# Products of two constants into an unread PSUM bank, in the table stages, the relational output and the attention outputs

## The chip, the cores and the metric

One NeuronCore of a Trainium2 chip runs the whole program. The metric is the device time of one execution in microseconds (us); lower is better.

## The reference

Four graph layers follow each other on 3125 nodes of width 32 and 100000 edges that are sorted by destination. Each layer is added to its input and layer-normalised:

```python
x = _layernorm(x + _L0_gnn_ref(x, Wq, Wk, Wv, Wo, edge_index))        # attention over edges, 4 heads
x = _layernorm(x + _L1_gnn_ref(x, weight, w_comp, self_loop_weight,
                               A1_w, A1_b, A2_w, A2_b, rel_emb, src, dst, edge_type))   # 86 relations, 16 bases
x = _layernorm(x + _L2_gnn_ref(x, edge_weight, src, dst, 3))          # three rounds of weighted sums
x = _layernorm(x + _L3_gnn_ref(x, edge_index, ..., Wl, bl, Wr, br, att, ...))   # 3 GATv2 layers, 8 heads of 32
```

In the layers that look at pairs of nodes, each node is first projected: `xl = x @ Wl + bl` for the source side and `xr = x @ Wr + br` for the destination side. For a GATv2 layer these are 8 x 32 = 256 columns each; the output of such a layer is the mean over heads of `sum(alpha * xl[src])`.

## The kernel before

The program is a sequence of stages. Each stage is a block in which every engine has its own list of instructions; engines wait for each other by semaphores, and the next stage begins when all engines have finished the block. The 3125 nodes lie as NB = 25 blocks of 128 nodes (the partitions). All orders below are written out by hand; there is no scheduler.

**Table stages** (`tables`, run five times: t, r, g0, g1, g2). TensorE (PE) transposes x four blocks at a time (`turn`, line L497, a product with the identity into `psT`), ScalarE (ACT) copies the result to `XT` (L514), and then for each block PE makes two f32 products of `XT` with the weights (L506): the source side into one half of `psA` and the destination side into the other, two blocks in turn. ACT copies the first half to `big` (L2005, L1461, L1992). The second half goes to `rows`, by VectorE (DVE) in stages t and r (L2006, L1459), by ACT in g0 to g2 (L1993). SyncE sends `big` to HBM in four parts (L545). In g0 to g2 DVE follows with `self_logits`: for every four blocks it adds the two sides (L1823), makes the leaky ReLU (L1809), multiplies by the attention vector (L1812) and reduces (L1815), and at the end it subtracts once for all blocks (L1829). The contraction of the products is 33 rows (32 features and a row of ones), 32 rows in stage t. Widths are 64 and 32 columns in t, 32 and 32 in r, 264 and 264 in g0 to g2. An f32 product is two instructions of PE in the trace.

**Relational output** (`relational_out`, once). For each block PE transposes four 128x128 parts of the sums and one of 32 columns into `psA` (L1422, L1424), one block ahead; ACT copies them to `work` (L1445, L1446); PE multiplies them with `w1b` and `w1s`, 32 columns wide, into `psC` (L1434, L1436); DVE takes the result (L1452).

**Attention output** (`attention_out`, once in each of g0 to g2). DVE computes the normalising factors (L1854 to L1866) and signals `shifted` after L1858. It then forms the normalised sums in four parts of 6, 6, 6 and 7 blocks (L1870, L1871, L1873), each part signalling `sums`. PE works on pairs of blocks: `turn` transposes the pair's four 128x128 parts into `psT` (L1904), ACT copies them to `work` (L1889), PE multiplies by `w3o`, 32 columns wide, into `psC` (L1916), ACT copies that out (L1880). `turn` runs one pair ahead.

Between the table stage and the output of each layer lie the edge stages (`logits`, softmax, weighted sums). They are not changed. The stage `dense_fill` of the third layer already issues, after each of its products (L1669), a 128x512 bf16 product of `ident_b` with `iota_b` into a bank that nobody reads (L1671).

Of the kernel before, what the change touches and what calls it, by code (L numbers as in the profile page):

```python
# [468 lines left out]

def tables(nc, m, name, sources, dests, tab, side, layer=None):

    gat = layer is not None
    w = m.table_d[name].shape[1]
    out = m.big[:, 0:NB * w].rearrange("p (b w) -> p b w", b=NB)
    rows = sources.shape[0]
    steps = [range(b, min(b + 4, NB)) for b in range(0, NB, 4)]  # L480
    parts = 4
    ends = [(n + 1) * NB // parts for n in range(parts)]

    def bank(b, n):
        return m.psA[:, b % 2, n * 512:n * 512 + (sources, dests)[n].shape[1]]

    with ExitStack() as ctx:
        s = Stage(nc, f"tab_{name}")
        block = ctx.enter_context(nc.Block())

        @block.tensor
        def _(pe):
            def turn(n):
                need(pe, s("copied"), n - 1)
                for b in steps[n]:
                    at = (b - steps[n][0]) * P
                    ins = nc.tensor.transpose(m.psT[0:D, n % 2, at:at + P], m.X[:, b, :], m.ident[:, :])  # L497
                ins.then_inc(s("turned"), 1)
            turn(0)
            for b in range(NB):  # L500
                if b % 4 == 0 and b // 4 + 1 < len(steps):
                    turn(b // 4 + 1)
                pe.wait_ge(s("copied"), b // 4 + 1)
                for n, (weights, read) in enumerate(((sources, "tab"), (dests, "side"))):
                    need(pe, s(read), b - 1)
                    nc.tensor.matmul(bank(b, n), m.XT[0:rows, b * P:(b + 1) * P], weights, start=True,  # L506
                                     stop=True).then_inc(s(f"made_{read}"), 1)

        @block.scalar
        def _(act):  # L510
            def copy_turned(n):
                bs = steps[n]
                act.wait_ge(s("turned"), n + 1)
                nc.scalar.copy(m.XT[0:D, bs[0] * P:(bs[-1] + 1) * P], m.psT[0:D, n % 2, 0:len(bs) * P]  # L514
                               ).then_inc(s("copied"), 1)
            copy_turned(0)
            for b in range(NB):
                if b % 4 == 0 and b // 4 + 1 < len(steps):
                    copy_turned(b // 4 + 1)
                act.wait_ge(s("made_tab"), b + 1)  # L520
                tab(out[:, b, :], bank(b, 0)).then_inc(s("tab"), 1)
                if gat:
                    act.wait_ge(s("made_side"), b + 1)
                    side(b, bank(b, 1)).then_inc(s("side"), 1)

        @block.vector
        def _(dve):
            if w > W3 or name == "r":
                lo = W3 + H3 if w > W3 else 0
                nc.vector.tensor_copy(out[:, :, lo:lo + D], m.X[:, :, :]).then_inc(s("x"), 1)  # L530
            else:
                dve.sem_inc(s("x"), 1)
            if gat:
                self_logits(nc, m, s, dve, layer)
            for b in range(0 if gat else NB):
                dve.wait_ge(s("made_side"), b + 1)
                side(b, bank(b, 1)).then_inc(s("side"), 1)

        @block.sync
        def _(sp):  # L540
            view = m.table_d[name].rearrange("(b p) w -> p b w", p=P)
            sp.wait_ge(s("x"), 1)
            for lo, hi in zip([0] + ends, ends):
                sp.wait_ge(s("tab"), hi)
                sp.dma_start(view[:, lo:hi, :], out[:, lo:hi, :]).then_inc(s("out"), 16)  # L545
            sp.wait_ge(s("out"), 16 * parts)
# [862 lines left out]
def relational_out(nc, m):  # L1409
# [3 lines left out]
    with ExitStack() as ctx:  # L1413
# [4 lines left out]
        def _(pe):  # L1418
# [8 lines left out]
            for b in range(NB):  # L1427
                if b + 1 < NB:
                    turn(b + 1)
                pe.wait_ge(s("copied"), 2 * (b + 1))  # L1430
                need(pe, s("y"), b - 1)
                zt = m.work[:, b % 2, :]
                for q in range(nq):
                    nc.tensor.matmul(m.psC[:, b % 2, 0:D], zt[:, q * P:(q + 1) * P], m.w1b[:, q, :], start=(q == 0),  # L1434
                                     stop=False)
                nc.tensor.matmul(m.psC[:, b % 2, 0:D], zt[0:D, 512:512 + P], m.w1s[:, :], start=False, stop=True  # L1436
                                 ).then_inc(s("made"), 1)

        @block.scalar
        def _(act):  # L1440
# [391 lines left out]
def attention_out(nc, m, l):  # L1832
# [8 lines left out]
    with ExitStack() as ctx:  # L1841
# [54 lines left out]
        def _(pe):  # L1896
            def turn(n):
# [3 lines left out]
                for j, b in enumerate(pairs[n]):  # L1901
                    for q in range(2):
                        at = j * W3 + q * P
                        ins = nc.tensor.transpose(m.psT[:, n % 2, at:at + P], acc[:, b, q * P:(q + 1) * P],  # L1904
                                                  m.ident[:, :])
                ins.then_inc(s("turned"), 1)
            turn(0)
            for n, bs in enumerate(pairs):
                if n + 1 < len(pairs):
                    turn(n + 1)  # L1910
                pe.wait_ge(s("copied"), n + 1)
                need(pe, s("z"), n - 1)
                for j in range(len(bs)):
# [159 lines left out]
```

## Time and profile before

| | |
|---|---|
| median of 3 runs | 10178.83 us (10178.52 to 10178.95) |
| the profiled execution | 10187.42 us, span 10185.9 us |
| PE busy | 7426.0 us (73%) |
| PE loading weights | 5623.9 us (55%) |
| DVE busy | 6327.8 us (62%) |
| POOL busy | 4728.1 us (46%) |
| ACT busy | 908.0 us (9%) |
| mean granted TensorE clock | 0.874 |

The span is the time from the first to the last instruction in one profiled execution. "PEclk" is the share of TensorE's full clock of 2.4 GHz that was granted; in a short stretch it is 1.00 (2.4 GHz) or 0.50 (1.2 GHz), and a value between them means that the clock changed inside the stretch. Weight loads (PEld) overlap the matmuls (PE). The busy shares of the whole span say little of the changed stages, which together are a small part of it; they have to be read stage by stage.

### The profile page before, as it was taken

The numbers are of one execution on the slowest core, as the hardware profiler recorded it, in microseconds if no ns is written. First come the engines' busy times: TensorE is split into PE (matmuls) and PEld (weight loads), VectorE is DVE, ScalarE is ACT, GpSimd is POOL, SyncE is SP. The second block draws the span as 40 slices with busy tenths as digits, with TensorE's granted clock in tenths as the row PEclk, the third lists the DMA queues.
The fourth block names the chain that finished last, engine by engine and source line by source line (L and its number), as shares of the span: only waits on it lengthen the run. The fifth ranks groups of instructions, "written<-read, shape, count | busy, mean of one in ns | idle before, by whom it ended". The sixth has DMA issues, their size and how long they took to land. (4 is left out here: it accounts for less than half of the span.)

```text
span 10185.9 us, 183728 instructions
## 1 busy us (share of the span) xinstructions
PE 7426.0 (73%) x30867; PEld 5623.9 (55%) x30868; DVE 6327.8 (62%) x11370; ACT 908.0 (9%) x3742; POOL 4728.1 (46%) x5670
## 2 busy tenths in 40 slices
PE   1899979788887877765666638966663896666388
PEld 1899969666666444421444426744442674444266
DVE  1333355666664677730577776767777676777777
ACT  0222211000001000000000001200000120000012
POOL 0777600555552788830477730047773005777300
PEclk9999999899997999976688869968886987888698
DMA  9444454444442233367477757457775645677564
GB/s 46 111 119 120 119 152 156 117 119 119 116 117 59 90 110 110 110 236 271 134 182 183 186 146 165 139 137 182 183 187 144 167 132 146 180 186 189 143 167 124
DMA packets 1717751, 1476.66 MB, mean 145 GB/s; under 512 B 951333, under 2 KB 1311774, under 8 KB 1717140
## 3 DMA queue, kind: packets, MB, share of 16 engines
q1 hardware_dynamic: 1437876, 949.34, 35.0%
q0 software_dynamic: 163424, 409.43, 16.0%
q10 hardware_dynamic: 116352, 116.73, 3.3%
q8 instruction: 42, 0.69, 0.0%
q14 instruction: 57, 0.47, 0.0%
HBM read 1110.02 MB, written 364.81 MB: 145 GB/s over the span
## 5 line engine op out<-in xcount | busy, mean ns | idle before, releaser
L620 POOL DMA_INDIRECT gx<-table_g,gi x2352 | 2226.4, 947 | 925.9 <-issue 662.7
L859 PE MATMUL ps<-rows,oh 128*128 x5280 | 1784.5, 478 | 1121.2 <-POOLq L597 763.2
L859 PEld LDWEIGHTS ps<-rows,oh 128*128 128x128 f32 x5280 | 1144.7, 234 | 1721.9 <-POOLq L597 987.5
L1196 PE MATMUL ps<-work,oh 128*128 128x273 f32 (+1 forms) x7040 | 1661.6, 405 | 295.7 <-DVE work L1150 260.6
L1196 PEld LDWEIGHTS ps<-work,oh 128*128 128x128 f32 x7040 | 1359.6, 228 | 596.7 <-issue 234.2
L1150 DVE TENSOR_TENSOR work<-rows,xl 128x1024 f32<-128x1024 f32 (+1 forms) x880 | 872.7, 992 | 470.5 <-PE ps L1196 270.6
L1383 PE MATMUL ps<-work,oh 128*128 128x272 f32 x3520 | 973.5, 436 | 245.8 <-issue 232.4
L736 DVE TENSOR_TENSOR work<-gx,ps 128x768 f32<-128x768 f32 x660 | 629.8, 954 | 809.7 <-PE ps L861 743.6
L593 POOL COPY gi<-src_i 128x16 int32 (+1 forms) x250 | 51.2, 205 | 2323.2 <-ACTq L694 1671.7
L620 POOL DMA_INDIRECT gx<-table_r,gi x784 | 742.0, 946 | 611.6 <-DVE work L1324 378.6
L1383 PEld LDWEIGHTS ps<-work,oh 128*128 128x128 f32 x3520 | 727.0, 212 | 413.9 <-issue 255.3
L1658 POOL TENSOR_SCALAR oh<-gx,lin 128x196 f32<-128x196 f32 x1176 | 885.7, 771 | 81.7 <-POOL lin L1654 81.7
L620 POOL DMA_INDIRECT gx<-table_t,gi x784 | 741.0, 945 | 276.6 <-issue 223.9
L1669 PE MATMUL ps<-oh 128*128 128x196 f32 x2352 | 671.6, 367 | 217.9 <-DVE oh L1636 214.5
L721 DVE TENSOR_REDUCE red<-work 128x32 f32<-128x1024 f32 x660 | 800.4, 1213 | 0.0
L1669 PEld LDWEIGHTS ps<-oh 128*128 128x128 f32 x2352 | 376.2, 189 | 613.2 <-DVE big L1629 578.1
L1324 DVE TENSOR_TENSOR work<-ps,gx 128x2048 f32<-128x2048 f32 x220 | 504.2, 2292 | 207.0 <-issue 189.9
L745 DVE SCALAR_TENSOR_TENSOR work<-work,ps 128x768 f32<-128x768 f32 x660 | 625.5, 948 | 0.0
L1629 DVE SCALAR_TENSOR_TENSOR big<-big,gx,ps 128x196 f32<-128x196 f32 x1176 | 491.8, 418 | 201.1 <-PE ps L1669 190.2
L671 DVE TENSOR_TENSOR big<-big,ps 128x273 f32 (+2 forms) x1100 | 486.5, 442 | 107.1 <-issue 73.8
L1636 DVE TENSOR_SCALAR oh<-iota_row,big 128x128 f32<-128x128 f32 x1176 | 480.5, 409 | 38.7 <-PE ps L1669 0.2
L861 PE MATMUL ps<-gx,ident 128*128 x1320 | 477.7, 450 | 0.0
(291 smaller groups left out, 7834.5 us busy)
## 6 DMA issues: line engine op xcount, KB each, us to landing
oh<-hot_d SPq DMA_DIRECT2D x880, 256.0 KB, 2.7
oh<-hotT_d SPq DMA_DIRECT2D x660, 256.0 KB
big<-dense_d SPq DMA_DIRECT2D x96, 784.0 KB
dense_d<-big SPq DMA_DIRECT2D x588, 98.0 KB
dense_d<-big ACTq DMA_DIRECT2D x588, 98.0 KB, 1.7
hotT_d<-ohT SPq DMA_DIRECT2D x220, 256.0 KB
hot_d<-oh ACTq DMA_DIRECT2D x220, 256.0 KB, 2.0
ohT<-hotT_d SPq DMA_DIRECT2D x220, 256.0 KB, 2.9
```

The source lines that it names most:

```text
L620: pool.indirect_dma_start(m.gx[:, u, k, 0:w], None, table, bass.IndirectOffsetOnAxis(m.gi[:, odd, u * K + k:u * K + k + 1].bitcast(U32), 0 ...
L721: nc.vector.tensor_reduce(m.red[:, half, :], prod(half).rearrange("p (k c) -> p k c", c=dh), AX.X, ALU.add).then_inc(s("reduced"), 1)
L736: nc.vector.tensor_tensor(tiles[:, 0:apart, :], rows[:, 0:apart, 0:cols], sums[:, 0:apart, :], ALU.add).then_inc(s("summed"), 1)
L745: nc.vector.scalar_tensor_tensor(out=tiles[:, 0:apart, :], in0=tiles[:, 0:apart, :], scalar=0.0, in1=att.to_broadcast([P, apart, cols]), o ...
L859: ins = nc.tensor.matmul(to, turned, rows, start=True, stop=not adds)
L1150: nc.vector.tensor_tensor(o, p, x, ALU.mult).then_inc(s("rhs"), 1)
L1196: ins = nc.tensor.matmul(sums(u), m.oh[:, u, k, :], rhs(u % 2)[:, k, :], start=(k == 0), stop=(k == K - 1))
L1324: nc.vector.tensor_tensor(rhs(half)[:, :, 0:NBASE * D].rearrange("p k (b c) -> p k b c", b=NBASE), scales[:, half, :, :].unsqueeze(3).to_b ...
L1383: ins = nc.tensor.matmul(m.psA[:, half, n * 512:n * 512 + ACC1 // 2], m.oh[:, slot, k, :], rhs(half)[:, k, n * ACC1 // 2:(n + 1) * ACC1 // 2],
L1629: nc.vector.scalar_tensor_tensor(out=sums[:, u, :], in0=sums[:, before(u), :], scalar=m.v_keep[:, bass.ds(v, 1)], in1=m.ps[:, u, 0:HIS], o ...
L1658: nc.gpsimd.tensor_scalar(his[:, u, :], m.hi_no[:, :], numbers[:, u:u + 1], None, ALU.is_equal).then_inc(s("high"), 1)
L1669: nc.tensor.matmul(m.ps[:, u, 0:HIS], spots[:, u, :], his[:, u, :], start=True, stop=True).then_inc(s("made"), 1)
```

## The change

A function `filler` issues one bf16 product of two constants, the identity with rows of the numbers 0 to 127, up to 128x512 (with `chunks` = K = 4 it is 512 columns). It writes a PSUM bank that nobody reads in that stage, waits for nothing and signals nothing.

- In every table stage there are six of them after the first `turn`, and one at each block before the wait for `XT`: 31 per stage, 155 in all.
- In the relational output there is one before the wait of each block and one after its products: 50.
- In each attention output PE first waits for `shifted`, then issues twelve, and then two per pair between the next `turn` and the wait for the copy: 12 + 26 = 38 per stage, 114 in all.

```diff
+def filler(nc, m, bank, chunks):
+
+    nc.tensor.matmul(bank[:, 0:chunks * P], m.ident_b[:, :],
+                     m.iota_b[:, :].unsqueeze(1).to_broadcast([P, K, P])[:, 0:chunks, :], start=True, stop=True)
+
@@ tables
             turn(0)
+            for n in range(6):
+                filler(nc, m, m.psC[:, n % 2, :], K)
             for b in range(NB):
                 if b % 4 == 0 and b // 4 + 1 < len(steps):
                     turn(b // 4 + 1)
+                filler(nc, m, m.psC[:, b % 2, :], K)
                 pe.wait_ge(s("copied"), b // 4 + 1)
@@ relational_out
                 if b + 1 < NB:
                     turn(b + 1)
+                filler(nc, m, m.psT[:, 0, :], K)
                 pe.wait_ge(s("copied"), 2 * (b + 1))
...
                 nc.tensor.matmul(m.psC[:, b % 2, 0:D], zt[0:D, 512:512 + P], m.w1s[:, :], start=False, stop=True
                                  ).then_inc(s("made"), 1)
+                filler(nc, m, m.psT[:, 1, :], K)
@@ attention_out
                 ins.then_inc(s("turned"), 1)
+            pe.wait_ge(s("shifted"), 1)
+            for n in range(12):
+                filler(nc, m, m.psA[:, n % 2, :], K)
             turn(0)
             for n, bs in enumerate(pairs):
                 if n + 1 < len(pairs):
                     turn(n + 1)
+                for c in range(2):
+                    filler(nc, m, m.psA[:, c, :], K)
                 pe.wait_ge(s("copied"), n + 1)
```

## Rows read from the trace of the kernel before

**Rows 1.** Windows: length; PE, PEld, DVE, ACT, POOL busy; granted clock; DMA share; GB/s.

```profile
206.30:237.40 31.10, 28.26 (x125) 24.59 (x125) 4.79 (x25) 10.29 (x33) 0.01 (x1) 1.00 0.13 27
1768.20:1799.10 30.90, 28.20 (x125) 24.62 (x125) 5.78 (x26) 8.27 (x32) 0.00 (x0) 0.50 0.13 27
3191.50:3260.80 69.30, 68.71 (x375) 64.63 (x375) 4.79 (x25) 18.23 (x50) 0.00 (x0) 0.64 0.00 1
4858.10:4919.50 61.40, 51.82 (x125) 35.22 (x125) 31.79 (x30) 22.55 (x57) 0.00 (x0) 0.50 0.18 62
...
6587.90:6619.30 31.40, 31.13 (x150) 30.77 (x150) 16.07 (x9) 10.13 (x26) 0.00 (x0) 0.50 0.00 1
```

**Rows 2.** Timeline of g0: start, length in us, engine, line, operation [idle before].

```profile
4858.14 1.86 PE L497 MATMUL ps<-ident,X 128*32 128x128 f32 x8 [10.36 <-PEq L1982]
...
4859.93 7.41 PE L506 MATMUL ps<-w,XT 33*128 33x264 f32 x16
...
4867.86 1.23 DVE L1823 TENSOR_TENSOR work<-big,rows 128x1024 f32<-128x1024 f32 x1 [8.74 <-ACT rows L1993]
...
4919.07 0.37 DVE L1829 TENSOR_TENSOR self<-self,rows 128x200 f32<-128x200 f32 x1
```

**Rows 3.** Timeline of stage t, two groups of four blocks.

```profile
208.25 3.62 PE L506 MATMUL ps<-w,XT 32*128 32x64 f32 x16
...
212.77 3.62 PE L506 MATMUL ps<-w,XT 32*128 32x64 f32 x16
```

**Rows 4.** Windows with different clocks; the columns are those of group 1.

```profile
3191.50:3211.50 20.00, 19.66 (x158) 18.48 (x159) 1.92 (x10) 7.97 (x22) 0.00 (x0) 0.99 0.01 2
3212.00:3260.70 48.70, 48.55 (x217) 45.72 (x215) 2.79 (x15) 10.26 (x28) 0.00 (x0) 0.50 0.00 1
4922.50:4925.50 3.00, 2.91 (x6) 1.85 (x6) 0.00 (x0) 0.00 (x0) 2.39 (x3) 0.50 0.68 218
...
4927.80:4931.50 3.70, 3.70 (x9) 2.99 (x10) 1.34 (x4) 0.00 (x0) 2.79 (x4) 0.50 0.69 194
4931.60:4938.30 6.70, 3.55 (x14) 2.16 (x14) 4.35 (x7) 0.00 (x0) 4.92 (x6) 1.00 0.56 140
...
3361.50:3400.00 38.50, 31.38 (x130) 16.51 (x128) 30.54 (x86) 0.00 (x0) 33.53 (x54) 1.00 0.34 113
...
4859.90:4909.90 50.00, 50.00 (x118) 34.22 (x117) 21.64 (x19) 21.60 (x55) 0.00 (x0) 0.50 0.16 55
```

**Rows 5.** Timeline of PE in `dense_fill`, before and after the clock rose.

```profile
3359.91 0.63 PE L1671 MATMUL ps<-iota_b,ident_b 128*128 128x512 bf16 x1
3360.34 0.86 PE L1669 MATMUL ps<-oh 128*128 128x196 f32 x2
...
3361.75 0.38 PE L1671 MATMUL ps<-iota_b,ident_b 128*128 128x512 bf16 x1
3361.97 0.59 PE L1669 MATMUL ps<-oh 128*128 128x196 f32 x2
```

**Rows 6.** Timeline of the relational output, early and late.

```profile
3194.47 0.66 PE L1422 MATMUL ps<-ident,big 128*128 128x128 f32 x4
...
3196.31 0.66 PE L1422 MATMUL ps<-ident,big 128*128 128x128 f32 x4
...
3227.78 1.11 PE L1422 MATMUL ps<-ident,big 128*128 128x128 f32 x4
...
3231.14 1.11 PE L1422 MATMUL ps<-ident,big 128*128 128x128 f32 x4
```

**Rows 7.** Timeline of the first attention output.

```profile
6578.32 0.37 DVE L1858 TENSOR_TENSOR small<-big,small 128x200 f32<-128x200 f32 x1
...
6587.93 1.97 PE L1904 MATMUL ps<-ident,big 128*128 128x128 f32 x8 [12.14 <-DVE big L1873]
...
6603.72 1.09 PE L1904 MATMUL ps<-ident,big 128*128 128x128 f32 x4
...
6606.17 1.09 PE L1904 MATMUL ps<-ident,big 128*128 128x128 f32 x4
```

## The prediction, made before the changed kernel was run

> **What bounds the kernel now.** I read the windows of each changed stage first, because the edge stages between them are untouched. PE is busy for 28.26 of 31.10 us in stage t, 28.20 of 30.90 in r, 68.71 of 69.30 in the relational output, 51.82 of 61.40 in g0 (g1 and g2 read the same) and 31.13 of 31.40 in the first attention output (the other two alike) [rows 1]. So PE sets the pace in all nine stages, and their sum is 31.1 + 30.9 + 69.3 + 3 x 61.4 + 3 x 31.4 = 410 us, 4% of the span. Only g0 to g2 have a second bound close by: DVE starts at 4867.86, when four blocks are ready, and ends at 4919.44, 9.5 us after PE [rows 2, 4].
>
> Next, the clock in these windows. It is 0.50 in r, g0 and the attention output and 0.64 in the relational output. Stage t shows 1.00, but its sixteen products take 3.62 us and four blocks 4.52 us [rows 3], and its busy time is that of r at 0.50 [rows 1]; I read t as slow too, with the 1.00 being a record that had not begun.
>
> Third, what the clock is worth. In the relational output a block takes 3196.31 - 3194.47 = 1.84 us at 1.00 and 3231.14 - 3227.78 = 3.36 us at 0.50 [rows 4, 6].
>
> **Does a filler pass for work?** In dense_fill the same product takes 0.43 us to the next start at 0.50 and 0.22 at 1.00 [rows 5]. There the clock rose inside a run of alternating real and constant products, and held at 1.00 with PE busy 31.38 of 38.5 us [rows 4, 5]. So I take it that fillers count.
>
> **Does the clock rise?** Elsewhere it rose after 3.7 us of unbroken work and did not after 2.9 us [rows 4]. The start of a table stage after the change is an unbroken run: four transposes (8 take 1.86 us, so 0.85), six fillers (6 x 0.43 = 2.56), four transposes (0.85) and one filler (0.43), together 4.7 us. I take a rise in each of the five table stages, on average 4.4 us after the stage's start, between the 3.7 us that sufficed elsewhere and the end of the run. At either clock the products of the blocks then begin about there, since a faster clock shortens the fillers. The 33-row products alone never brought one: 50.00 us busy out of 50.00 at 0.50 in g0 [rows 4].
>
> Do the transposes in that run count? In the relational output two thirds of the streamed columns are transposes (five of 0.107 us per block against ten passes of 0.027), and the clock stayed at 1.00 for 20 us [rows 4, 6]; I take it that they do. The Trainium skill speaks against this: "TensorE: Matmul & The Clock Gate", Part 4 (PE-mode transpose), says that transposes do not count as PE activity in the same way. By the page the starting run would be its fillers alone, 2.56 us, and the third rival below would be the result.
>
> **Does it hold?** The nearest row is again the relational output: with 0.80 us of streaming in each block of 1.84 us it held 1.00 for 20 us and then fell, with no change in its pattern [rows 4, 6]. A pattern like that can go either way. With two fillers more per block it is denser than a stretch that nearly held by itself, so I expect it to hold throughout. Stages t and r have four fillers and four transposes, 0.86 + 0.43 us, in about 3.2 us: much as the relational output before, steadier. In g0 to g2 the same 1.29 us stand in about 4.9 us, and the other 3.5 are the 33-row products. If those weigh by their height, a quarter, g0 lies with t and r; if they weigh nothing, it is much thinner than the stretch that fell. This is the hinge of the forecast, and no row shows 33-row products at 1.00. I take the quarter, since a weight of nothing for work that has a quarter of the rows would be odd, and keep the other as a rival.
>
> **The change part by part, likeliest case.**
>
> *g0 to g2.* At 1.00 a block costs PE 0.88 us (16 instructions for four blocks take 7.41 us at 0.50, of which 7.04 are streaming and the rest the last one's latency; half of 7.04/4) plus a filler 0.22, plus a quarter of 0.43 for transposes: 1.2 us instead of 51.82/25 = 2.07 [rows 1, 2]. ACT needs 22.55/25 = 0.90 per block and stays behind it. PE then begins its products 4.4 us after the start instead of 1.8, has four blocks at 4.4 + 4.9 and DVE starts about 9.6 us in (before: 4867.86 - 4858.14 = 9.7). From there DVE bounds: its work is 31.79 less 0.99 for one copy = 30.8 us, plus 3.6 us of waiting for the second four blocks and 0.03 between each of 26 instructions, 35.3 in all. The stage lasts 45 us instead of 61.3: **16.1 us less, 48.4 in three**. The cover is DVE: were self_logits free, PE's own gain would be larger by little.
>
> *t and r.* Here weight loads pace PE, 0.213 us each at 0.50 (3.41 of the 4.52 us), and halve. Four blocks: 1.71 loads, 0.43 transposes, 0.25 of gap and four fillers, each adding its 0.22 and its own load of about 0.05, less 0.11 for the next load hidden under it, up to the whole 0.27: 3.05 to 3.45, I take 3.2 instead of 4.52. Over 25 blocks 26.4 becomes 20.0, less 2.5 for the later start: **3.9 less each, 8 together** (bounds 5 to 10).
>
> *Relational output.* It enters at 1.00. With two fillers a block costs 1.84 + 2 x (0.16 to 0.27) = 2.16 to 2.38; I take 2.25 x 25 + 1.3 for the start = 57.6 against 69.1: **11.5 less** (8 to 14).
>
> *Attention outputs.* PE waits 12.14 us for the first sums [rows 7], so the twelve fillers (12 x 0.43 = 5.1 us at most) cost nothing. But they start at `shifted`, after L1858, at about 6578.8, and are over by 6584; the first `turn` comes at 6587.93. The twelve therefore stop 4 us before they could help, and the clock will be back at 0.50, as it was after the 12.14 us of idling. In the loop a pair takes 6606.17 - 6603.72 = 2.45 us, of which four transposes stream 0.85 and eight passes 0.43. Two fillers fill it up further, but weight loads still interrupt it in every pair, and the runs that raised the clock in [rows 4, 5] were unbroken. I take it to stay at 0.50. Then two fillers cost 0.85 less the load hidden under each, about 0.75 per pair; DVE's parts come well ahead of PE, so all of it shows: 12.5 pairs, **9.5 us more each, 28.5 in three** (bounds 8 to 10.6 each).
>
> The wait on `shifted` delays nothing: behind it is only `turn(0)`, which waits longer. Fillers write banks that no engine reads in the stage, so no semaphore comes later through them but by PE's order.
>
> Sum: -48.4 - 8 - 11.5 + 28.5 = -39.4 us. The profiled execution took 10187.42 us (span 10185.9), 8.6 above the median; -39.4 on the median 10178.83 gives **10139 us**.
>
> **Rivals.**
> 1. *The attention outputs warm up too.* For it: two `turn`s and two fillers stand back to back at the start, 2.56 us. Against it: that is below the 2.9 us that did not suffice. A pair would fall to 1.28 of loads, 0.2 of gap and 0.3 of fillers, 1.75 us; the last part of the sums is ready at about 16 us after the first `turn`, and four pairs follow: 23 us instead of 31.4, 8.5 less each. Against my case 3 x (8.5 + 9.5) = 54 less: **10085 us**.
> 2. *The clock rises in g0 to g2 and falls again in mid-stage,* because 33-row products weigh too little, or small gaps between blocks thin them out. It would hardly rise again, since then fillers are 0.43 in every 2.19 us. After four fast blocks, 21 cost 9.7/4 us: PE ends 60 us in, and DVE's tail of 9.5 follows: 70 instead of 61.3, 8.4 more each, 25 in three. The stage loses from a fall before about the 11th block (4.4 + 1.2 n + 2.43 (25 - n) + 9.5 = 61.3); with the attention outputs' 28.5 the whole loses from one before about the 13th. Sum: 25 - 8 - 11.5 + 28.5 = +34: **10213 us, slower.** This is the rival on the other side.
> 3. *The clock never rises in a table stage* (transposes or fillers don't count). g: 2.6 later and 0.35 per block, 11.4 more each, 34. t and r: 2.6 and 0.33 per block, 11 each, 22. The relational output gains as before if fillers count: -11.5. Attention +28.5. Sum +73: **10252 us**. If fillers counted for nothing at all, add about 25.
> 4. *Mixed:* one or two of the three g stages fall back, each worth 16.1 + 8.4 = 24.5: 10164 or 10188, no change within 0.2% or a little less.
>
> **Chances.** The likeliest case 0.46, rival 1 0.14, rival 2 0.17, rival 3 0.09, mixed 0.14. About 0.2% (20 us) is what a measurement of this kernel tells from no change. Faster: 0.46 + 0.14 and some of the mixed, 0.64; same 0.14 (the mixed, and sizes off); slower 0.22. The range runs from rival 1 to rival 2, 10085 to 10213; the likeliest case's own is 10125 to 10155.
>
> **What would show it.** In g0: clock 0.50 for some 3 to 6 us, then 1.00 to the last product; ACT's copies of the sources 1.1 us apart; L1823 to L1829 back to back, the stage 45 us long. Wrong if the clock falls inside. In t and r: four blocks in 3.2 us. In the relational output: 1.00 throughout, 2.25 us from one first transpose to the next. In the attention outputs: 0.50 at the first `turn` and after, 3.2 us per pair; if 1.00 stands there, rival 1 holds. The edge stages should be as before to a few us; the clock at their start is 0.50 either way, since DVE's tail leaves PE idle.

## The result: slower, and what the profile after shows

The changed kernel takes 10275.14 us in the median of 4 executions (10265.48 to 10294.86), the kernel before 10178.89 us (10178.52 to 10201.42, 4 executions on the same chip). The ratio is 1.0092, 95% interval 1.0079 to 1.0106: slower. The prediction said 10139 us and a range up to 10213 us. The profiled execution has a span of 10275.1 us, 89.2 more than that of before. Its mean granted clock is recorded as 0.804 instead of 0.874, but that compares two different records and not two clocks: the trace of before holds no entry ahead of 1746.9 us and counts that stretch as 1.00, while that of after begins at 208.0 us and has 0.50 from 218.2 to 1750.8 us. From 460 to 1240 us PE's busy time is the same in both (745.0 and 746.7 us). So the mean clocks say nothing of the change.

Each stage lasts from its first instruction to the first of the next one:

| stage | before, us | after, us | change | predicted |
|---|---|---|---|---|
| t | 31.1 | 40.9 | +9.9 | -3.9 |
| r | 33.7 | 49.2 | +15.4 | -3.9 |
| relational output | 69.5 | 56.5 | -13.0 | -11.5 |
| g0, g1, g2, each | 61.6 | 73.0 | +11.4 | -16.1 |
| attention output, each of three | 42.8 | 53.6 | +10.7 | +9.5 |
| dense_fill (untouched) | 1076.3 | 1096.2 | +19.9 | 0 |

The nine changed stages add 78.6 us, dense_fill (an unchanged stage with a section of its own below) 19.9, and the rest, mostly the edge stages, takes back 9.3.

The windows that answer to [rows 1], and two inside g0 (window; length; PE, PEld, DVE, ACT, POOL busy; granted clock; DMA share; GB/s):

```profile
205.00:245.90 40.90, 38.16 (x156) 24.80 (x156) 4.80 (x25) 10.27 (x33) 0.00 (x0) 0.66 0.10 21
1772.90:1821.50 48.60, 43.60 (x156) 28.02 (x156) 5.74 (x26) 8.36 (x32) 1.21 (x3) 0.54 0.11 23
3212.50:3268.90 56.40, 56.15 (x425) 50.47 (x425) 4.81 (x25) 18.23 (x50) 0.00 (x0) 1.00 0.01 1
4884.60:4957.30 72.70, 64.03 (x156) 31.85 (x156) 31.80 (x30) 22.61 (x57) 0.00 (x0) 0.57 0.15 52
6622.70:6665.00 42.30, 41.86 (x176) 36.23 (x176) 16.04 (x9) 10.15 (x26) 0.00 (x0) 0.50 0.00 0
4887.70:4897.90 10.20, 10.20 (x43) 5.71 (x41) 1.22 (x1) 5.70 (x14) 0.00 (x0) 1.00 0.01 2
4897.90:4948.00 50.10, 50.10 (x107) 24.71 (x105) 20.68 (x18) 15.79 (x41) 0.00 (x0) 0.50 0.16 55
```

PE is busy without a break in g0 till its last product, and yet the clock is at 1.00 for 10.2 us only, from 3.1 us after the stage's start, and at 0.50 for the 50.1 us that follow. Only the relational output stays at 1.00. The timeline of PE in g0 (start, length, line, operation; L474 is the product of constants) answers to [rows 2]:

```profile
4884.60 1.01 PE L503 MATMUL ps<-ident,X 128*32 128x128 f32 x4 [10.36 <-PEq L1998]
4885.41 2.58 PE L474 MATMUL ps<-iota_b,ident_b 128*128 128x512 bf16 x6
...
4888.25 0.38 PE L474 MATMUL ps<-iota_b,ident_b 128*128 128x512 bf16 x1
...
4889.65 0.39 PE L474 MATMUL ps<-iota_b,ident_b 128*128 128x512 bf16 x1
...
4891.06 0.39 PE L474 MATMUL ps<-iota_b,ident_b 128*128 128x512 bf16 x1
...
4894.32 0.38 PE L474 MATMUL ps<-iota_b,ident_b 128*128 128x512 bf16 x1
...
4902.50 0.63 PE L474 MATMUL ps<-iota_b,ident_b 128*128 128x512 bf16 x1
...
4905.12 0.61 PE L474 MATMUL ps<-iota_b,ident_b 128*128 128x512 bf16 x1
```

These lines give the price of one product of constants, a filler. At 1.00 a block takes 4891.06 - 4889.65 = 1.41 us. Its own products are worth 0.88 (the prediction's half of 7.04/4), so the filler costs 0.53, not 0.22. At 0.50 it takes 4905.12 - 4902.50 = 2.62 us against 1.76: 0.86, not 0.43. With the transposes, four blocks take 4894.32 - 4888.25 = 6.07 us, 1.52 each instead of 1.2.

PE's weight loads (PEld) show where the rest goes. Here, in after, the filler's load starts together with the filler at 4905.12, after 0.68 us without a load:

```profile
4905.12 0.10 PEld L474 LDWEIGHTS ps<-iota_b,ident_b 128*128 128x128 bf16 x1 [0.68 <-issue]
4905.66 0.50 PEld L515 LDWEIGHTS ps<-w,XT 33*128 33x128 f32 x2 [0.43 <-issue]
```

In stage t a block at 0.50 now takes 230.67 - 229.12 = 1.55 us. In [rows 3] it took 0.89, since four blocks and the first transposes after them start 211.80 - 208.25 = 3.55 us apart:

```profile
229.12 0.63 PE L474 MATMUL ps<-iota_b,ident_b 128*128 128x512 bf16 x1
...
230.67 0.61 PE L474 MATMUL ps<-iota_b,ident_b 128*128 128x512 bf16 x1
```

In the relational output ([rows 6]) a block takes 2.22 us, all of it at 1.00:

```profile
3217.89 0.60 PE L1431 MATMUL ps<-ident,big 128*128 128x128 f32 x4
...
3220.11 0.60 PE L1431 MATMUL ps<-ident,big 128*128 128x128 f32 x4
```

In the first attention output ([rows 7]) the twelve fillers stop 5 us before the first turn. They did bring the clock to 1.00, from 6618.2 to 6621.6 us, but PE had nothing to do then; the first turn at 6622.70 runs at 0.50, and a pair takes 6630.19 - 6626.88 = 3.31 us:

```profile
6613.57 4.13 PE L474 MATMUL ps<-iota_b,ident_b 128*128 128x512 bf16 x12 [3.01 <-DVEq L1870]
6622.70 1.97 PE L1915 MATMUL ps<-ident,big 128*128 128x128 f32 x8 [5.00 <-DVE big L1884]
...
6626.88 1.09 PE L1915 MATMUL ps<-ident,big 128*128 128x128 f32 x4
...
6630.19 1.09 PE L1915 MATMUL ps<-ident,big 128*128 128x128 f32 x4
```

### The profile page after: what moved, and what is told of

The parts are those of the page before. It is cut to its first block and busy times, and to the rows that moved or that the text cites. A ratio compares the mean times of both kernels' runs of the same rounds, so it can differ in the third digit from the quotient of the medians.

```text
span 10275.1 us, 184366 instructions
## 1 busy us (share of the span) xinstructions
PE 7513.1 (73%) x31186; PEld 5581.4 (54%) x31187; DVE 6305.9 (61%) x11370; ACT 907.7 (9%) x3742; POOL 4748.5 (46%) x5670
## 5 line engine op out<-in xcount | busy, mean ns | idle before, releaser
L868 PE MATMUL ps<-rows,oh 128*128 x5280 | 1760.4, 473 | 1134.0 <-POOLq L606 763.2
L1680 PEld LDWEIGHTS ps<-oh 128*128 128x128 f32 x2352 | 350.8, 188 | 658.0 <-DVE big L1640 481.9
L868 PE MATMUL ps<-rows,ohT 128*128 x1760 | 419.3, 402 | 52.0 <-ACT ohT L813 25.1
```

The lines of the kernel that those rows point to most:

```text
L868: ins = nc.tensor.matmul(to, turned, rows, start=True, stop=not adds)
L1680: nc.tensor.matmul(m.ps[:, u, 0:HIS], spots[:, u, :], his[:, u, :], start=True, stop=True).then_inc(s("made"), 1)
```

## The experiments

My theory after the result had two parts: PE being busy is not enough for 1.00, the height of its products (rows of the contraction) matters too; and a filler is dear where its height differs from its neighbours', because the weight load is then not hidden behind the product before it. The rival was that fillers as such, by type or number, cost this much.

### The three parts alone

Each kernel keeps the fillers of one place and leaves out the others.

```diff
 # e1_tables: no fillers in relational_out and attention_out
 # e2_outr:   no fillers in tables and attention_out
 # e3_attn:   no fillers in tables and relational_out
```

> Fillers in the five table stages alone, none in the relational output and the attention outputs. By the stage lengths of the two profiles the table stages lost 9.9 (t), 15.4 (r) and 3 x 11.4 us (g0 to g2), and the logits after them gave back about 12. If each stage's fillers act by themselves, this kernel is 45 to 60 us slower than before, the clock in g0 to g2 stands at 1.00 for the first ten us or so and then falls for good. Rival: the loss depends on the others (a shifted position in the program, dense_fill's 20 us among them); then the sum differs from that by 15 us or more, and dense_fill, which is not changed, is again 1096 us long instead of 1076.

> Fillers in the relational output alone. The stage should be 56.5 us long with a clock of 1.00 throughout, instead of 69.5, so the kernel is 13 us faster (ratio 0.9987) if dense_fill stays at 1076 us. Rival: the fillers here are what turns dense_fill, the next but two stage, to 1096 us; then the kernel is 7 us slower than before.

> Fillers in the three attention outputs alone. Each should be 53.6 us instead of 42.8, the clock 0.50 from the first transpose on, 3.3 us per pair instead of 2.45: 32 us slower in all (ratio 1.0032). The twelve fillers ahead cost nothing. Rival: the stage's fillers cost less without the table stages' ones before them; not expected, as other stages lie between.

Measured against before on one chip: tables 1.0078 (1.0055 to 1.0101), relational output 0.9994 (0.9983 to 1.0005), attention outputs 1.0025 (1.0013 to 1.0036). The stages are those of the table above, except t at 48.9 and g1 at 78.9 us in e1_tables: in that g1 the clock stands at 1.00 for 3.4 us, and in t no rise is on record. The tables carry the loss: 80 us, against 45 to 60 expected, with dense_fill at 1097.0 us, the rival's side. The attention outputs cost 24 us where 32 were expected, with each stage at the expected 53.6. The relational output's stage gives its 13.0 us, but dense_fill takes 1097.2 us in the profile of that kernel and eats them; it takes 1076.3 in e3_attn.

### Height: the products over 128 rows, no fillers

```diff
-    m.XT = sb("XT", [D + 1, NP])
+    m.XT = sb("XT", [P, NP])           # rows beyond D + 1 are zero, set once
-    m.w3 = sb("w3", [D + 1, 3, 2, ROW3])
+    m.w3 = sb("w3", [P, 3, 2, ROW3])   # w0 and w1 alike
```

> The kernel before, without a filler, but its table products contract over all 128 rows: XT and the weights are padded with zero rows. The arithmetic is the same. Theory: the clock did not stay up in g0 to g2 because a product over 33 rows weighs by its height. Then here the clock rises within about 7 us of the start of g0, g1 and g2 by the products alone and stays, a block costs PE 0.88 us, DVE bounds, and each stage is about 44 us instead of 61.6: 50 us faster in all (ratio 0.995). t and r stay at 0.50, as their products are narrow and weight loads stand between: no change there. Rival: rows of zeros, or the number of rows, do not matter to the clock: all stages as before, ratio 1.000.

0.9934 (0.9909 to 0.9959): faster. Windows of e4_rows128, g0 and the part of it at 1.00:

```profile
4852.20:4894.60 42.40, 27.64 (x125) 22.27 (x125) 31.75 (x30) 22.13 (x57) 0.00 (x0) 0.82 0.25 90
4857.20:4884.40 27.20, 22.64 (x111) 18.65 (x109) 21.02 (x18) 19.92 (x53) 0.00 (x0) 1.00 0.40 140
```

The same 125 instructions that stayed at 0.50 for 50 us in [rows 4] now bring the clock to 1.00 five us into the stage, with no filler at all, and it stays there for 27.2 us, past PE's last product (over at 4879.8). g1 and g2 show the same. Adding rows of zeros changes neither the columns streamed nor the order. It does remove the change of height between transposes and products, and so PE's exposed loads there; e5_fill33 below, with more streaming between 33-row products and 0.50 all the same, speaks against that as the cause. The stage lasts 42.7 instead of 61.6 us, and DVE bounds it: it works without a wait from 4863.80 to the end. t and r stay at 0.50 (t by its times, r on record) and still lose 2.1 us each; that this is the one height of transposes and products is argued. relation_walk, which also reads `XT`, is 6.6 us shorter; I did not follow that up. Against this, the relational output, unchanged here, took 77.0 us instead of 69.5: its 1.00 ended 10.6 us into the stage instead of 19.7.

### A filler of the height of its neighbours

```diff
-    nc.tensor.matmul(bank[:, 0:chunks * P], m.ident_b[:, :],
-                     m.iota_b[:, :].unsqueeze(1)...
+    nc.tensor.matmul(bank[:, 0:chunks * P], m.ident_b[0:D + 1, :],
+                     m.iota_b[0:D + 1, :].unsqueeze(1)...
```

> Fillers in the table stages alone, as in the run with only those, but each over 33 rows instead of 128 (33 rows of the identity, 512 columns). In the changed kernel a filler made a block of g0 2.62 us long at 0.50, 0.86 more than its products' 1.76, and 1.40 at 1.00, 0.52 more than 0.88, while the filler itself is 0.43 and 0.22. Theory: the rest is the weight load ahead of it and the one after it, which are exposed where the height changes between 33 and 128 rows. Then here the block is 2.19 us at 0.50 (0.43 more). And the clock stays at 0.50 in all five table stages, as nothing in them but the transposes has the full height. Rival: the exposed loads come from the change between f32 and bf16 (the block is again 2.6 us), and the clock rises as before, so that columns alone count.

e5_fill33 has fillers of 33 rows in the tables only; e6_rows_fill has fillers of 128 rows between products of 128 rows. Both were run once, for the profile:

```diff
 # e6_rows_fill: the edit of e4_rows128, and the table stages' fillers of the change
```

> The padded products over 128 rows and the fillers of the table stages together. Theory of the height: no load is exposed, so in g0 a filler costs 0.22 us and a block is 1.10 to 1.15 us long at 1.00; the clock rises in all five table stages and holds. g0 to g2 are bound by DVE, 42 to 45 us as without fillers. t and r rise to 1.00, about 0.65 us per block, 24 to 27 us against 29.0 and 31.6 with the padding alone. Rival: the fillers' cost has another cause and stays at 0.5 us per block; g0 takes 47 us or more and t and r are longer than with the padding alone.

Timelines of e5_fill33 in g0 (33 rows beside 33), in t (33 beside 32) and in r (33 beside 33):

```profile
4926.10 0.63 PE L474 MATMUL ps<-iota_b,ident_b 33*128 33x512 bf16 x1
...
4928.28 0.63 PE L474 MATMUL ps<-iota_b,ident_b 33*128 33x512 bf16 x1
...
217.52 0.60 PE L474 MATMUL ps<-iota_b,ident_b 33*128 33x512 bf16 x1
...
219.04 0.60 PE L474 MATMUL ps<-iota_b,ident_b 33*128 33x512 bf16 x1
...
1799.92 0.61 PE L474 MATMUL ps<-iota_b,ident_b 33*128 33x512 bf16 x1
...
1801.04 0.61 PE L474 MATMUL ps<-iota_b,ident_b 33*128 33x512 bf16 x1
```

A block of g0 takes 2.18 us: 0.42 for the filler, the streaming alone. Its load now starts 0.44 us ahead of it, while the product before it still runs:

```profile
4927.84 0.15 PEld L474 LDWEIGHTS ps<-iota_b,ident_b 33*128 33x128 bf16 x1
4928.28 0.76 PEld L515 LDWEIGHTS ps<-w,XT 33*128 33x128 f32 x2 [0.29 <-issue]
```

In r a block takes 1.12 us, in t 1.52, where both took 0.89 in before: one row of difference makes the filler 0.63 instead of 0.23. That t's products are 64 columns wide and r's 32 is not the reason: at equal heights (e6_rows_fill) a block takes 0.58 us in both. Other unequal pairs than 33 or 32 beside 128 and 33 beside 32 were not run, so whether every difference exposes the load is open. The clock is 0.50 in all of g0 to g2, which take 73.5 us each: the cheaper filler alone gains nothing on the 73.0 of the change. In e6_rows_fill the filler costs 0.22 at 1.00 (block 1.10 us, products 0.88):

```profile
4880.71 0.38 PE L478 MATMUL ps<-iota_b,ident_b 128*128 128x512 bf16 x1
...
4881.81 0.38 PE L478 MATMUL ps<-iota_b,ident_b 128*128 128x512 bf16 x1
```

So both parts of the theory stand, and type (bf16 beside f32) falls as the cause of the price. Fillers over padded products pay in t (23.9 us) and r (25.8), where without them the clock stays at 0.50 (29.0 and 31.6); in g0 to g2 they only cost: 45.5 us against 42.4.

### Attention outputs: can the clock be brought in and held?

```diff
-            for n in range(12):
+            for n in range(28):
...
-                for c in range(2):      # e7_bridge: none in the loop; e10_hold: one per pair
-                    filler(nc, m, m.psA[:, c, :], K)
```

> Attention outputs alone: 28 fillers after the wait on the shifted factors instead of 12, to reach to the first sums, and none in the loop. Theory: the twelve did nothing because they ended some 4 us before the first transpose. Here the clock is 1.00 at the first transpose, a pair takes about 1.4 us instead of 2.45, PE waits for DVE's sums, and the stage is 33 to 36 us long instead of 42.8. Rival: without fillers in the loop the clock falls again after a few pairs, as in the relational output before (38 to 42 us).

> Kernel of before plus, in the attention outputs alone, 28 products of constants after the shift and one (instead of none) per pair in the loop. The run with 28 and none in the loop reached 1.00 at the first turn and lost it after the second pair. Theory (what holds the clock is full-height work with few gaps): one product of 0.22 us per pair of about 1.65 us of turns and products holds 1.00; a pair takes 1.65 to 1.9 us instead of 2.45, and the stage 34 to 37 us instead of 42.8; all three save 18 to 26 us, the ratio is 0.9975 to 0.9985. Rival (the pairs are gated by ScalarE's copies, and the gaps lose the clock anyway): the clock falls after three to five pairs, a pair then takes 2.45 + 0.4 us, and the stage takes 44 to 47 us: 5 to 12 us slower in all.

PE in e7_bridge:

```profile
6579.46 7.90 PE L474 MATMUL ps<-iota_b,ident_b 128*128 128x512 bf16 x28 [3.01 <-DVEq L1865]
6588.59 1.09 PE L1910 MATMUL ps<-ident,big 128*128 128x128 f32 x8 [1.23 <-DVE big L1879]
...
6598.71 1.09 PE L1910 MATMUL ps<-ident,big 128*128 128x128 f32 x4
...
6601.17 1.09 PE L1910 MATMUL ps<-ident,big 128*128 128x128 f32 x4
```

The first turn is at 1.00, but the clock falls 2 us after it and a pair takes 2.45 us again: 42.1 instead of 42.8 us, where 33 to 36 were expected (one execution). In e10_hold, with one filler per pair, 1.00 lasted for nine pairs in the first output. It fell as PE waited 1.28 us for DVE's last part, but it had outlasted a wait of 1.32 us at 6610.25, so what ended it isn't shown (windows of the first output and of the loop of the second):

```profile
6605.00:6621.00 16.00, 13.18 (x108) 12.26 (x108) 15.90 (x9) 6.88 (x17) 0.00 (x0) 1.00 0.00 0
8372.15:8405.00 32.85, 32.30 (x146) 30.61 (x147) 16.58 (x10) 9.16 (x22) 0.00 (x0) 0.50 0.00 0
```

The first output took 40.4 us, the other two 48.0: there the clock was still at 1.00 when the 28 fillers began, so they were over after 6.2 us instead of 7.9, and it fell in the 2.9 us of waiting that followed. At 1.00 PE is ahead of DVE, which is busy 15.90 of the 16.00 us. Ratio 1.0012 (1.0000 to 1.0025), the rival's side of my expectation. The best such stage of any run won 7.2 us (35.6, below), and a miss costs 5.

### dense_fill: who makes it 20 us longer?

No instruction of dense_fill is changed, but in the change and in e1_tables to e8_rows_outr it took 1096 to 1098 us in every kernel with fillers ahead of it, and 1076 to 1080 in before, e3_attn, e4_rows128 and e7_bridge. Its loop has one of two steady rhythms, 3.65 or 3.72 us per four visits, and 293 times 0.07 us is the difference. Theory 1 says that the place of PE's instructions decides between them, theory 2 that the first turns do. e9_shift adds 52 products of ones in the stage of constants; e12_start is e8_rows_outr with one more filler after dense_fill's first product.

```diff
+            for n in range(52):
+                nc.tensor.matmul(m.psT[:, n % 2, 0:P], m.ones[:, :], m.ones[:, :], start=True, stop=True)
```

> The padded products over 128 rows without fillers, and the fillers of the relational output. The two act in different stages and should add: 58 us for the padding's stages and 13 to 20 for the relational output (56.5 us against 69.5 to 77), so 70 us faster than before (ratio 0.993). Rival: dense_fill moves by its 20 us either way and hides a part; its length in the profile tells.

> Kernel of before plus 52 products of ones with ones in the stage of constants, where PE has nothing else to do; nothing is left out. dense_fill takes 1076.3 us in before and 1096 to 1097 us in every kernel so far that has products added ahead of it. Theory 1 (the place of PE's instructions, or their number, does it): dense_fill takes 1096 to 1097 us here too. Theory 2 (the loop has two steady rhythms, one of 3.65 us and one of 3.72 us per four visits, and the clock in its first microseconds settles which one it falls into): in before the clock drops to 0.50 with the first product and stays there for two records, in the kernels of 3.72 us it is still 1.00 for the first 2.4 us; the 52 products stand 3000 us ahead and leave that alone, so the first turns look like those of before and dense_fill takes 1076 to 1077 us. The whole: theory 1 about 20 us above before, theory 2 within 5 us of it.

> Padding and the relational output's products (0.9943, dense_fill 1097.2 us) with one more product of constants after the very first product of dense_fill, some 0.22 to 0.43 us once in a stage of 1097 us. Theory 2 (two steady rhythms, set by the first turns): so small a push at the start can send the loop into the other rhythm, 3.65 us per four visits, and then dense_fill takes 1077 us, 20 us less for 0.2 us more; that it does not go over at this push is possible too (chance even), then it takes 1097. Theory 1 (place of the instructions in memory): 1097 us, since the loop has moved by one instruction only; a length strictly between the two would speak against both.

e8_rows_outr (padding and the relational output's fillers) gave 0.9943 (0.9924 to 0.9961) with dense_fill at 1097.2 us. e9_shift (run once) has 1097.0 us, as theory 1 said, but e10_hold, with nothing ahead of dense_fill, has 1096.1, and e11_rows_tr, with 112 fillers ahead of it, 1076.4: the place of the code does not settle it. e12_start stayed at 1096.1 us (0.9932, 0.9912 to 0.9952). So the unchanged kernel was profiled twice more.

> The kernel of before, unchanged, profiled once more: does one kernel show both rhythms of dense_fill? Its executions on the last chip lie in two heaps, 10181.5 to 10196.8 and 10210.7 to 10216.6 us, some 22 us apart, which is the price of 293 groups of four visits at 3.72 instead of 3.65 us. Theory 2 (chance of the first turns): dense_fill is 1076 to 1080 or 1096 to 1098 us, nothing between, and 1.00 instead of 0.50 at its first products goes with the longer one. Theory 1 (the code): 1076 to 1077 us each time.

> The same once more, as for e13_again: 1076 to 1080 or 1096 to 1098 us by theory 2, with about even chances; two profiles may show the same one by luck, and then the question stays as open as the heaps of times leave it.

POOL's timeline in the middle of dense_fill, first in e13_again:

```profile
3903.23 0.19 POOL L1654 COPY lin<-big 128x4 f32 x1 [0.17 <-POOL oh L1658]
3903.69 3.02 POOL L1658 TENSOR_SCALAR oh<-gx,lin 128x196 f32<-128x196 f32 x4 [0.28 <-POOL lin L1654]
3906.89 0.19 POOL L1654 COPY lin<-big 128x4 f32 x1 [0.17 <-POOL oh L1658]
```

and in e14_again2, the same kernel:

```profile
3902.38 0.19 POOL L1654 COPY lin<-big 128x4 f32 x1 [0.17 <-POOL oh L1658]
3902.84 3.09 POOL L1658 TENSOR_SCALAR oh<-gx,lin 128x196 f32<-128x196 f32 x4 [0.28 <-POOL lin L1654]
3906.10 0.19 POOL L1654 COPY lin<-big 128x4 f32 x1 [0.17 <-POOL oh L1658]
```

3.66 against 3.72 us; the stages take 1079.9 and 1097.0 us. The kernel of before has both rhythms, so the 19.9 us between two single profiles do not show a cost of the change. Whether the change makes the long rhythm likelier is open: leaving out e9_shift and the kernels with doubled products below, it came in seven of the eight profiles with fillers ahead of dense_fill (all but e11_rows_tr) and in two of the seven without. The groups of instructions show the two meeting differently on POOL and DVE:

```profile
L1658 POOL TENSOR_SCALAR oh<-gx,lin 128x196 f32<-128x196 f32 x1160 | 876.2, 774 | 80.7 <-POOL lin L1654 80.7
L1636 DVE TENSOR_SCALAR oh<-iota_row,big 128x128 f32<-128x128 f32 x1159 | 479.9, 414 | 38.3 <-PE ps L1669 0.2
```

in e13_again, and in e14_again2:

```profile
L1658 POOL TENSOR_SCALAR oh<-gx,lin 128x196 f32<-128x196 f32 x1141 | 880.0, 785 | 79.3 <-POOL lin L1654 79.0 <-PE ps L1669 0.3
L1636 DVE TENSOR_SCALAR oh<-iota_row,big 128x128 f32<-128x128 f32 x1140 | 389.9, 342 | 37.9
```

In the short rhythm DVE's comparison takes 414 ns and POOL's 774, in the long one 342 and 785. I read this as the two meeting at a different point of the loop and slowing each other there, with POOL bounding the loop; no run separates them. The Trainium skill ("GPSIMD Engine Reference", 8. Key points) says that GpSimd shares its SBUF interfaces with VectorE; these rows agree. Which rhythm comes goes in part with the first turns. In before, e3_attn, e4_rows128 and e11_rows_tr the clock fell to 0.50 at the stage's start, PE's first product and the filler behind it start 0.79 us apart (3355.88 and 3356.67 in before), and the short rhythm followed; in twelve profiles they start 0.40 apart (3359.53 and 3359.93 in e13_again), at 1.00, and the long one followed in ten (not in e7_bridge and e13_again). Two more kernels imitate the slow start:

```diff
-                nc.tensor.matmul(m.ps[:, RING + u, :], m.ident_b[:, :], filler, start=True, stop=True)
+                for _ in range(2 if isinstance(i, int) else 1):    # the first 8 visits
+                    nc.tensor.matmul(m.ps[:, RING + u, :], m.ident_b[:, :], filler, start=True, stop=True)
```

> The kernel of before with two products of constants instead of one in the first 8 visits of dense_fill. In all four profiles in which PE stood at 0.50 in the first turns the loop fell into the rhythm of 3.65 us, in eight of nine in which it began at 1.00 into that of 3.72 us. Two products at 1.00 take as long as one at 0.50 (0.43 us), so the first turns should look like those at 0.50 whatever the clock. Theory (the pace of PE's first turns settles it): 1076 to 1080 us in the profile and the executions lie in one heap, the median 0 to 12 us below before. Rival (the phase of DVE against POOL, not PE's pace, settles it): both heaps remain, ratio 0.999 to 1.001.

> The pinned kernel of before once more, on the same chip as e17_after_slow8, to stand beside it: all its executions in one heap, dense_fill 1076 to 1080 us, 0.9989 of before as in the last run, plus or minus 0.001.

> The changed kernel with dense_fill held to its faster rhythm, by two products of constants instead of one in its first 8 visits. What is left between it and the kernel of before in the same rhythm is the change alone. From the stages: t +9.9, r +15.4, g0 to g2 +34.2, attention outputs +32.1, relational output -13.0, logits behind them 0 to -12: 66 to 79 us above the pinned kernel of before (ratio of the two 1.0065 to 1.0078). If dense_fill's 20 us do come from the change after all, its rhythm stays 3.72 here and the difference is 86 to 99 us (1.0085 to 1.0097).

dense_fill takes 1077.3 and 1080.8 us in e15_slow8 and e18_before_slow8, and 1079.7 and 1076.4 us in e17_after_slow8 and e16_best (below). Four short ones of four is what the theory says, but in the first two the clock fell to 0.50 at the stage's start of itself, and there the short rhythm came without doubled products too (four of four). Only the other two, whose stage began at 1.00, test them. As a gain it isn't shown: 0.9989 (0.9978 to 1.0001) and 0.9997 (0.9988 to 1.0006). The times say a little more: on the chip of the first, before lay in two heaps (eight of 15 at 10165 to 10183 and seven at 10194 to 10202 us) and e15_slow8 with its ten in one (10163 to 10182); on that of the second before had no such heaps. So the doubled products probably hold the short rhythm, and it isn't proven.

With the doubled products in both, on one chip, the changed kernel takes 10248.63 us (10241.04 to 10257.60) and the one of before 10172.95 (10164.73 to 10189.54): 75.7 us, 1.0074. Against before without them, the ratio is 1.0069 (1.0055 to 1.0083). This is the best figure for the change alone. It lies inside the 66 to 79 us expected, in part by luck, since the stages are not those of that sum. In its profile g0 to g2 take 78.8 us each, with 1.00 for 3.4 us instead of 10.2, and the first attention output 35.6 us: there the clock did rise, and a pair takes 1.71 us.

```profile
6611.89 0.63 PE L1916 MATMUL ps<-ident,big 128*128 128x128 f32 x4
...
6613.60 0.64 PE L1916 MATMUL ps<-ident,big 128*128 128x128 f32 x4
```

This is my first rival, with its 1.75 us per pair, in one of the nine such stages of three profiles (after, e3_attn, e17_after_slow8).

### The parts that pay, together

e11_rows_tr has the padding, the relational output's fillers and the tables' fillers in t and r alone; e16_best adds the two fillers per visit at dense_fill's start.

```diff
+            for n in range(6 if name in ("t", "r") else 0):
+                filler(nc, m, m.psC[:, n % 2, :], K)
...
+                if name in ("t", "r"):
+                    filler(nc, m, m.psC[:, b % 2, :], K)
```

> Table products over 128 rows (padding by zero rows), the relational output's products of constants, and those of the table stages in t and r alone; not in g0 to g2, not in the attention outputs. From the stages of the runs so far: t 23.9 and r 25.8 us (31.1 and 33.7 in before), g0 to g2 42.5 each (61.6), relational output 56.5 (69.5), relation_walk -6.6, dense_fill +20 if it falls into the slower rhythm again, logits about -5 to +8. Against the padding with the relational output's products (0.9943) that is 11 us less: 0.993, time about 55 to 75 us below before. With dense_fill in the faster rhythm it would be 0.991.

> Padding to 128 rows, the relational output's products and those of the tables t and r (ratio 0.9914 as measured), with the doubled products in the first 8 visits of dense_fill. By the theory dense_fill stays at 1076 to 1080 us in every execution: 0.990 to 0.992. By the rival it has both heaps again and stays at 0.9914 plus or minus 0.001.

0.9914 (0.9896 to 0.9931) and 0.9908 (0.9890 to 0.9927), which these intervals don't tell apart; e16_best takes 10088.90 us against 10182.65 on its chip. Both are faster than the kernel of before and the change. Windows of t, r, the relational output and g0 in e16_best:

```profile
210.60:233.70 23.10, 18.95 (x157) 16.88 (x155) 7.18 (x30) 8.59 (x33) 1.28 (x3) 0.95 0.18 36
1761.80:1787.60 25.80, 18.99 (x151) 16.69 (x149) 5.86 (x26) 7.22 (x31) 2.52 (x4) 0.90 0.26 55
3171.80:3227.80 56.00, 54.40 (x414) 49.10 (x413) 5.86 (x27) 18.47 (x49) 0.00 (x0) 1.00 0.01 1
4824.10:4866.10 42.00, 26.93 (x125) 21.83 (x125) 31.04 (x28) 22.08 (x57) 0.00 (x0) 0.83 0.26 91
```

## Why the prediction was wrong

- **What bounds, and whether the clock rises: right.** PE set the pace in the changed stages. In the profile after the clock rose in all five table stages, 3.0 to 5.2 us after the start (4.4 taken). It isn't certain to: stage t of e1_tables, with the same fillers, took 48.9 us. In e5_fill33, with fillers of 33 rows, it did not rise in g0.
- **The price of a filler in the tables: wrong.** The step took 0.22 and 0.43 us, with the load hidden as in dense_fill [rows 5], where both products have 128 rows. Beside 33 rows it is 0.53 and 0.86; e5_fill33 and e6_rows_fill show 0.42 and 0.22 again at equal heights. In a stage at 0.50 this alone is 25 x 0.43 = 11 us more than the fillers' streaming.
- **"Does it hold": wrong, and the larger error.** "I take the quarter" was the hinge. The clock fell in the seventh block of g0, before the eleventh that rival 2 names as the point from which the stage loses. e4_rows128 shows the cause: over 128 rows the same products keep 1.00 to PE's end with no filler. How much a 33-row product weighs is not measured; that it is too little here, beside the gaps that the exposed loads leave, is. How much of it is their height and how much those gaps isn't separated in the changed kernel itself. t and r, for which no such doubt was held, fell too, after 10.2 and 3.4 us at 1.00. An estimate of the two errors, from the rows of after: held at 1.00 with 1.52 us a block, PE would end 42 us in (3.9 + 25 x 1.52), and the stage, with the 8.6 us that DVE takes after PE's end, some 51. So of the 28 us between the forecast 45 and the measured 73.0, the price makes about 6 and the fall, with the dearer filler at 0.50, about 22.
- **Sum for g0 to g2:** +34.2 instead of -48.4 us, 82.6 off. (By its own terms the forecast stage was 9.6 + 35.3 = 44.9 us, so 16.4 less and not 16.1; the slip is small.) It is rival 2, 73.0 us per stage where that said 70, and the nearness is partly luck: the clock fell two to three blocks later than that sum took, but a slow block cost 2.81 us (four in 4913.73 - 4902.50) and not 2.43. **t and r:** +25.3 instead of -8, 33.3 off, where rival 3 (+22) is nearest.
- **Relational output: right.** -13.0 for -11.5, a block 2.22 for 2.25 us. But the stage without fillers has 66.2, 69.5 or 77.0 us by profile (the last in e4_rows128 and e6_rows_fill), as its 1.00 ended 23.6, 19.7 or 10.6 us in, so its gain is 10 to 20 us by what it is compared with. That transposes help to hold the clock fits, since it stayed at 1.00 through 25 blocks in which they are most of the real work, but it isn't shown: two fillers stood in each block. The Trainium skill's "TensorE: Matmul & The Clock Gate", Part 4 (PE-mode transpose), says that transposes don't count as PE activity in the same way; no run here has transposes alone, so none decides it.
- **Attention outputs: right.** +10.7 for +9.5 each, a pair 3.31 for 3.2 us. Two fillers cost their full streaming, 2 x 0.43 = 0.86 per pair and not 0.75: no load was saved under them. Rival 1 is no fiction either, as the one stage of nine shows.
- **Range:** rival 2 had +34 with t and r at -8. Had their failure been taken with it, as one cause asks for (33 of the 44 us between it and the 78.6 of the stages), the upper end would have been some 10250 us. Rival 3, at 10252 us, lay outside the range with its chance of 0.09, and the chances themselves don't add up: "slower 0.22" is less than the 0.17 + 0.09 = 0.26 of rivals 2 and 3.
- **dense_fill's 19.9 us:** no step spoke of it. The kernel of before shows both lengths too, so they aren't shown to be the change's. The change's own effect is about 76 us, and that too lies beyond the forecast's range (10178.83 + 76 = 10255 us).

## What to carry to other kernels

Before spending instructions on warming TensorE, look at the height of the real products: zero rows up to 128 cost no column and did here what 31 fillers per stage could not (61.6 to 42.4 us in g0 to g2). Between products of its own height a filler cost its streaming at most; beside 33-row products it cost twice that or more (0.86 for 0.43, 0.53 for 0.22). And profile the unchanged kernel more than once before a stage's difference is put down to a change.

## What had not been expected of the hardware

- TensorE's granted clock does not go by PE being busy alone: 50 us without a gap at 0.50 with products of 33 rows (before), 27.2 us at 1.00 with the same products over 128 rows (e4_rows128).
- How long 1.00 lasts varies between executions of the same instructions: 19.7 us into the relational output of before and 23.6 in e13_again, the same kernel; 10.2 us in g0 of after and 3.4 in that of e17_after_slow8.
- In all pairs of heights that were run (33 and 32 beside 128, 33 beside 32), a weight load is exposed where consecutive products differ in height, even by one row (a filler costs 0.63 in t and 0.23 us in r of e5_fill33). The Trainium skill's "TensorE: Matmul & The Clock Gate", Part 3 (The mechanism), lists that a load overlaps a running product only when their row groups differ; here it is hidden at equal height and exposed at unequal, so the measurement decides against that line.
- A loop on several engines can lock into one of two rhythms, 3.65 and 3.72 us per four visits, and keep it for a millisecond (e13_again and e14_again2, one kernel).
